# A constant mask written once a layer, and five pieces of work placed sooner at the seams of a three-stage kernel

## The reference

```
qkv = shift(x) @ wqkv;  q, k = l2norm, scale, rotate        # 8 heads of 64
sim[i, j] = q_i . k_j, and -max where i < j                 # causal mask
x = x + softmax(sim) @ v @ wo
h = layernorm(shift(x)) @ w1 + b1                           # 256 -> 2 * 682
x = x + (a * gelu(g)) @ w2 + b2                             # 682 -> 256
```

## Time and profile before

| what | value |
|---|---|
| time, median of 3 runs | 2665.61 us (2664.37 to 2666.09) |
| the profiled execution | 2666.19 us; its span 2664.4 us |
| mean granted TensorE clock | 0.992 |
| busy: PE, PEld, DVE, ACT, POOL | 97%, 84%, 72%, 64%, 54% |
| PE idle over the span | 73.7 us |

### The profile page before, as it was taken

The page is one execution under the profiler, slowest core; times in us unless marked ns, Lnnn a source line. Parts: engine busy times, 40 slices in busy tenths (PEclk is TensorE's granted clock), DMA queues, the critical chain, the costliest instruction groups (busy, mean ns, idle before and its releaser), DMA issues.

```text
span 2664.4 us, 71388 instructions
## 1 busy us (share of the span) xinstructions
PE 2590.7 (97%) x25088; PEld 2225.2 (84%) x25088; DVE 1919.9 (72%) x3779; ACT 1703.1 (64%) x4184; POOL 1426.1 (54%) x1512
## 2 busy tenths in 40 slices
PE   7999999979999999999999998999999999999998
PEld 5888888768888888887888887888888888888887
DVE  7777777668888778786555556887788887666664
ACT  4666666658778777774444445877777877444442
POOL 7888888567777776662000006777777665000000
PEclk9999999989999999999999999999999999999999
DMA  2111111111111111112111111111111111222221
GB/s 48 37 48 38 43 38 35 42 45 39 50 41 47 41 39 38 57 50 70 56 49 59 53 36 43 40 49 41 49 39 39 40 59 36 79 76 74 78 77 40
DMA packets 167250, 130.39 MB, mean 49 GB/s; under 512 B 24870, under 2 KB 165320, under 8 KB 167093
## 3 DMA queue, kind: packets, MB, share of 16 engines
q1 hardware_dynamic: 164789, 119.81, 14.7%
q0 software_dynamic: 2304, 8.47, 1.1%
HBM read 77.47 MB, written 50.33 MB: 48 GB/s over the span
## 4 chain that ended last, share of the span: by engine, by line
PE 70%; DVE 12%; ACT 11%; issue 5%; POOL 1%; DMA 1%; DVEq 0%; ACTq 0%; SPq 0%; POOLq 0%
ACT attn_E L1103 8%; PE const_banks L1393 6%; PE const_banks L1394 6%; PE const_banks L1395 6%; PE const_banks L1401 3%; PE const_banks L1403 3%; PE const_banks L1402 3%; DVE attn_neg_top L1305 3%; DVE attn_ss L1295 3%; DVE attn_rot_b L1276 3%; PE const_banks L1416 3%; PE const_banks L1415 3%; PE const_banks L1414 3%; PE const_banks L510 3%; PE const_banks L525 3%
## 5 line engine op out<-in xcount | busy, mean ns | idle before, releaser
L1103 ACT ACTIVATE attn_E<-const_banks,attn_nbias,attn_rn 128x128 f32<-128x128 f32 x1024 | 453.5, 462 | 135.7 <-DVE attn_nbias L1310 135.7
L1014 POOL TENSOR_TENSOR attn_qk<-attn_rot_a,attn_rot_b 128x1024 f32<-128x1024 f32 x128 | 303.6, 2372 | 348.9 <-issue 296.7
L1001 POOL TENSOR_TENSOR ffn_rstd<-ffn_var,const_neg_half 128x4 f32<-128x4 f32 x32 | 32.3, 1010 | 669.5 <-DVE ffn_var L1200 669.5
L1401 PE MATMUL const_banks<-weights_w_hi,attn_xT_hi 128*128 128x512 f32 x768 | 316.2, 412 | 4.9 <-ACT attn_sq L1138 4.6
L1403 PE MATMUL const_banks<-weights_w_hi,attn_xT_lo 128*128 128x512 f32 x768 | 304.9, 397 | 0.0
L1402 PE MATMUL const_banks<-weights_w_lo,attn_xT_hi 128*128 128x512 f32 x768 | 304.6, 397 | 0.0
L1221 DVE SCALAR_TENSOR_TENSOR ffn_gated<-const_banks,weights_b_col,ffn_gate 128x512 f32<-128x512 f32 (+1 forms) x192 | 143.7, 748 | 213.7 <-ACT ffn_gate L1081 206.9
L1393 PE MATMUL const_banks<-ffn_xT_hi,ffn_w_hi 128*128 128x512 f32 x704 | 282.2, 401 | 3.4 <-DVE ffn_gated L1221 3.4
L1394 PE MATMUL const_banks<-ffn_xT_lo,ffn_w_hi 128*128 128x512 f32 x704 | 278.7, 396 | 0.0
L1395 PE MATMUL const_banks<-ffn_xT_hi,ffn_w_lo 128*128 128x512 f32 x704 | 278.3, 395 | 0.0
L1081 ACT ACTIVATE ffn_gate<-const_banks,weights_b_col 128x512 f32<-128x512 f32 x160 | 110.3, 689 | 217.4 <-PE const_banks L1395 217.1
(11 more groups left out here) (179 smaller groups left out, 8001.9 us busy)
## 6 DMA issues: line engine op xcount, KB each, us to landing
attn_x_res<-xa SPq DMA_DIRECT2D x128, 128.0 KB, 4.8
xb<-attn_x_new SPq DMA_DIRECT2D x128, 128.0 KB, 1.7
ffn_x_<-xb SPq DMA_DIRECT2D x128, 128.0 KB
h<-ident_h SPq DMA_DIRECT2D x64, 128.0 KB, 1.7
xa<-ident_n SPq DMA_DIRECT2D x64, 128.0 KB, 1.7
attn_x_<-xa SPq DMA_DIRECT2D x128, 64.0 KB
xa<-ffn_x_new SPq DMA_DIRECT2D x16, 512.0 KB, 3.3
ffn_add<-h SPq DMA_DIRECT2D x16, 512.0 KB, 5.0
```

The lines of the kernel that those rows point to most:

```text
L1014: pool.tensor_tensor(qk[:, slot].rearrange("p a n -> p (a n)"), rot_a[:].rearrange("p a h d -> p (a h d)"), rot_b[:].rearrange("p a h d -> ...
L1103: last = act.activation(E[:, r, i], ps_s[:, r, i * P:(i + 1) * P], ACT.Exp, bias=nbias[:, r, i:i + 1], scale=rn[:, slot, h:h + 1], accum_o ...
L1401: pe.matmul(out_, xT_hi[:, slot, k], w.w_hi[:, k, cols], start=(k == 0), stop=False)
```

## The change

Six edits. (1) The mask for queries 0 to 63 is written in full (4 x 128 keys) only in step 2 of a layer; in all later steps only the first 64 keys of each head are written again. (2) On POOL in layer 0, `late(76)` moves from ahead of step 2 into step 1, between the products of the keys (L1025) and the power for the queries (L1027), so ahead of the load of w1. (3) Row 3 of layer 1 is loaded in the feed-forward step GROUPS + 1, with row 2. (4) The second group's statistics, its `group_rstd` and its normalisation are placed in attention steps 64, 65 and 66. (5) `row_out` goes through the blocks in `ORDER` and for its first row waits for four pieces at its head, and for the fifth and the sixth where they are used. (6) Its last matmul is now the `h_lo` product of block 4.

```diff
-                if on(0) and not (layer and step in (0, 1, 2)):
+                if on(0) and not (layer and step in (0, 1, 2, 3)):
                     load_row(sp, layer, t, i, u)
...
-                    for row in (first, first + 1) if step == GROUPS else (first + 2,):
+                    for row in (first, first + 1) if step == GROUPS else (first + 2, first + 3):
                         load_row(sp, layer + 1, row, row // 4, row % 4)
...
-        def attention_pool(pool, layer, before=None):
+        def attention_pool(pool, layer, before=None, within=None):
...
+                    if within and step == 1:
+                        within()
                     pool.tensor_tensor(rn[:, slot, 0:HEADS], ssm[:, 0:HEADS], c["neg_half"][:, 0:HEADS], ALU.pow
                                        ).then_inc(s["rn_done"], 1)
...
                 if step == ROWS - 2:
                     group_rstd(pool, layer * GROUPS)
+                if step == ROWS + 1:
+                    group_rstd(pool, layer * GROUPS + 1)
...
-                if on(0) and step != 0:
+                if on(0) and step not in (0, 1):
                     group_rstd(pool, t)
...
+                if step == ROWS:
+                    group_statistics(dve, layer * GROUPS + 1, layer * GROUPS // 4, 1)
+                if step == ROWS + 2:
+                    group_normalise(dve, layer * GROUPS + 1, 1)
...
-                        if p == 0:
+                        if p == 0 and step != 1:
                             group_statistics(dve, t, i, u)
-                        if p == 1:
+                        if p == 1 and step != 1:
                             group_normalise(dve, t, u)
...
-            if r == 0:
-                need(pe, f["h_lo"], KH * (t - 1))
             tok = slice(r * P, (r + 1) * P)
-            for k in range(FULL):
-                pe.matmul(dst, h_hi[:, slot, k, tok], w.w2_hi[:, k], start=(k == 0), stop=False)
+            for p, k in enumerate(ORDER):
+                if r == 0 and p >= KH - 2:
+                    need(pe, f["h_lo"], KH * (t - 2) + p + 1)
+                elif r == 0 and p == 0:
+                    need(pe, f["h_lo"], KH * (t - 1) - 2)
+                if k == FULL:
+                    pe.matmul(dst, h_tail[:, slot, tok], w.w2_hi[:, FULL], start=False, stop=False)
+                    pe.matmul(dst, h_tail[:, slot, tok], w.w2_lo[:, FULL], start=False, stop=False)
+                    continue
+                pe.matmul(dst, h_hi[:, slot, k, tok], w.w2_hi[:, k], start=(p == 0), stop=False)
...
+                        if step == 2:
+                            pe.matmul(ps_s[0:HD, r], eye, rule.rearrange("p i n -> p (i n)"),
+                                      start=True, stop=False, skip_group_check=True)
+                        else:
+                            pe.matmul(ps_s[0:HD, r].rearrange("p (i n) -> p i n", n=P)[:, :, 0:HD], eye,
+                                      rule[:, :, 0:HD], start=True, stop=False, skip_group_check=True)
...
-                attention_pool(pool, 0, between(late, STEPS, also))
+                attention_pool(pool, 0, between(late, {**STEPS, 2: ()}, also), lambda: late(ROWS + 12))
```

More of the change, by code:

```diff
@@ L1409, in row_out @@
             need(pe, f["sum_done"], j - 1)
-            if r == 0:
-                need(pe, f["h_lo"], KH * (t - 1))
             tok = slice(r * P, (r + 1) * P)
-            for k in range(FULL):
-                pe.matmul(dst, h_hi[:, slot, k, tok], w.w2_hi[:, k], start=(k == 0), stop=False)
+            for p, k in enumerate(ORDER):
[8 more added lines that the diff above has]
+                pe.matmul(dst, h_hi[:, slot, k, tok], w.w2_hi[:, k], start=(p == 0), stop=False)
                 pe.matmul(dst, h_hi[:, slot, k, tok], w.w2_lo[:, k], start=False, stop=False)
-                pe.matmul(dst, h_lo[:, slot, k, tok], w.w2_hi[:, k], start=False, stop=False)
-            pe.matmul(dst, h_tail[:, slot, tok], w.w2_hi[:, FULL], start=False, stop=False)
-            pe.matmul(dst, h_tail[:, slot, tok], w.w2_lo[:, FULL], start=False, stop=True).then_inc(f["out_ps"], 1)
+                last = pe.matmul(dst, h_lo[:, slot, k, tok], w.w2_hi[:, k], start=False, stop=(p == KH - 1))
+            last.then_inc(f["out_ps"], 1)
         def queries_keys(pe, b, slot):
@@ L1528, in body @@
                         eye, rule = c["ident_b"][own, own], c["causal"][own]
-                        pe.matmul(ps_s[0:HD, r], eye, rule.rearrange("p i n -> p (i n)"),
-                                  start=True, stop=False, skip_group_check=True)
+                        if step == 2:
[4 more added lines that the diff above has]
+                                      rule[:, :, 0:HD], start=True, stop=False, skip_group_check=True)
                         pe.matmul(ps_s[HD:P, r].rearrange("p (i n) -> p i n", n=P)[:, :, HD:P], eye, rule[:, :, 0:HD],
```

## The result

The kernel after takes 2650.9 us in the median (2646.3 to 2653.52, 5 runs), the kernel before on the same chip 2665.95 (2664.37 to 2666.89, 5 runs): ratio 0.9945 (0.9933 to 0.9956), 14.7 us faster, with 12 to 18 as the interval. The prediction was 2645, its range 2633 to 2656. The profiled execution took 2650.90 us with a span of 2649.1; PE is busy for 2582.9 us, so its idle time fell from 73.7 to 66.2 us. That is about half of the gain; most of the rest is clock: the mean granted clock rose from 0.992 to 0.994, and 0.002 of the span is some 5 us.

What follows compares the result with a forecast made beforehand. PE was taken to bound the kernel, busy 97% of the span, with waits and low-clock stretches at the seams. Terms 0 + 5.0 + 4.0 + 6.5 + 1.7 + 3.1 = 20.3 us off 2666.2 gave 2645 after median adjustment, range 2633 to 2656.

Steps and rivals of the forecast that it cites:

- Edit 1: Attention rows' mask of queries 0 to 63: shortening it priced at 0 us, at most 13.
- The long mask lies beside that chain: Attention rows: the mask of queries 0 to 63 is hidden by the longer-running products of queries 64 to 127; 0 us.
- Edit 2: Start of layer 0's attention: POOL reaches the last row's work 4.4 us sooner; gain 5.0 us, bounds 1.2 and 6.0.
- Edit 3: Start of layer 1's attention: PE's 3.67 us wait for row 3's load goes; gain 4.0 us, bounds 2.0 and 5.3.
- Edit 4: Attention to feed-forward: PE's waits for the second group's statistics and normalisation go; 6.5 us in layer 0, 1.7 in layer 1.
- Edits 5 and 6: Kernel's end: most of PE's 3.04 us wait before the last `row_out` is filled; gain 3.1 us, bounds 1.5 and 3.4.
- M: Rival, attention rows: the mask is on PE's path and pays 13 us as well, 2632 us; chance 0.12.
- rival A: At the seams: half the gain is taken back by the next limit, 9.6 us won, 2656 us; chance 0.17.
- a seam's wait comes back under another name: At the seams: a sign that the forecast is wrong, a removed wait reappearing with another cause; no size given.
- the likeliest case: Whole kernel: the summed gain of 20.3 us holds, 2645 us, own range 2640 to 2651; chance 0.62.
- S: Rival, hardware loop: overhead of the looped rows grows; if doubled it costs 28 us, 2673 us; chance 0.03.
- N: Rival, whole kernel: an unseen wait takes up the gains wholly, 2663 us; chance 0.06.

Runs made afterwards that it cites:

- mask_only: The halved mask of queries 0 to 63 (edit 1) alone on the kernel before: 2662.79 us against 2664.33, ratio 0.9992.
- the long mask twice: Kernel before with the mask matmul of queries 0 to 63 (512 columns) issued twice in every row: 2671.34 us, ratio 1.0021.
- the short mask twice: Kernel before with the mask matmul of queries 64 to 127 (256 columns) issued twice in every row: 2665.7 us, ratio 1.0004.
- edit 4 alone: Only the second group's statistics and normalisation moved into attention's last steps, on the kernel before: 2658.1 us, ratio 0.9978.
- the load behind: Kernel after with layer 0's first load of w1 one step later on POOL, behind step 2's powers: 2646.99 us, ratio 0.9934.

## Why the prediction was right, and where it was off

The time is in the range and 5.9 us above the number. By parts:

- **Edit 1, 0.** Right in value, by a reason that is only half right: mask_only's row is 10.04 against 10.05, which by 126 rows is 1 to 2 us, and the interval of its 2.1 us includes zero. "The long mask lies beside that chain" is where it was weak: the tiles are coupled, as the long mask twice shows, but only after one product (two records), and the single long mask was short enough. And a longer chain did not cost what the prediction's account of it implies: 13.7 us were expected of the short mask twice and 1.1 (-1.3 to 3.7) measured. What hides an op of 0.1 us here is not the neighbouring tile alone, but also the slack of the row behind it.
- **Edit 2, 5.0; measured about 1** (0.6 to 1.1 in the trace once the late trace before is allowed for, 1.6 (-1.1 to 4.0) alone). This term failed: even its lower bound, 1.2, is hardly reached. The queue was followed rightly: L293 at 554.34, L1409 at 559.58, L1014 at 561.51 (forecast 554.7, 560, near 562). The failing step is "following each engine's queue by its present durations": L1301's present duration is 0.17 and it took 3.24, since in its new place it runs beside L1014. The Trainium skill (SBUF — State Buffer, Who interferes with whom) says that a DVE instruction with two SBUF inputs contends with a GpSimd instruction that reads SBUF; the ends at 563.96 and 563.92 agree with it, and so do 560.52 and 560.49. The clock adds to it: from 566 to 576 it was 0.66 in the kernel after, behind the 2.9 us wait.
- **Edit 3, 4.0; 4.2 in the trace, 6.1 (3.7 to 8.5) alone.** The wait went, and one of the two low stretches behind it; 1600 to 1650 has 0.97 of the clock in place of 0.93.
- **Edit 4, 6.5 in layer 0; 1.7 in the trace, 3.5 in that of edit 4 alone.** This and edit 2 are the terms that made the difference. The seam itself won 6.9 us, as forecast, but the step didn't ask what is late next: the sum was made up to 1227 and the next group, 14 us on, not looked at. Before, the third group's statistics started at 1236.36 with no wait for a load and PE had work; with the work before them some 8 us sooner, the loads and the slow normalisation became the path, and 5.2 us went back: PE's wait of 2.92 us and, from 1240.6, a stretch at the low clock (0.79 from 1238 to 1246). A small part too: of the 1.71 us wait for `ffn_gated`, 0.69 is left, because the split, now sooner, holds L1343 for 2.78 us ahead of it on DVE; the prediction saw the hold and looked only at who uses the low part, not at what is queued behind it. In layer 1, with nothing to split, edit 4 alone gives 1.9 against the forecast 1.7; the 2.9 in the kernel after has another 0.9 from a low stretch at 2248 that is in the trace before and not in this one.
- **Edits 5 and 6, 3.1; 3.1 in both traces, and 3.5 (1.1 to 5.9) alone.** The waits forecast as about 1.0 and 0.4 are 0.87 and 0.18, with no low stretch after them.

So rival A holds in its mechanism, a seam won and given back at the next limit, for two of the six terms: the sign "a seam's wait comes back under another name" was seen twice. The total, 14.7 us, lies midway between the likeliest case (20.3) and A (9.6). Some of it is luck. Edit 2 and edit 4 in layer 0 are short by some 9 us in the trace; what makes up for part of it is not in the sum: steady rows (1.4 us, in part edit 1's), the late trace before (1.3 to 1.8), and a low stretch less in layer 1 (0.9). S and N fell: the rows of the loop did not get longer, and the time did change. M fell with mask_only.

The kernel after spreads over 7.2 us (2646.3 to 2653.52) and before over 2.5. The granted clock of its five runs goes with the time: 0.996 at 2646.3, 0.994 at 2650.75 and 2650.9, 0.992 and 0.993 at 2651.92 and 2653.52; 0.001 of the span is 2.6 us. That the runs differ by a low stretch more or less is argued from the clock alone, and not tested.

## What to carry to other kernels

When a seam gets sooner by several us, go on past it to the next work that has not moved with it, here loads that are issued only after the previous stage; the gain is worth what that work allows. A duration read from a trace is good only for its neighbours: an operation of DVE moved beside one of POOL has to be costed anew, and so does one left in place when POOL's work is moved next to it. Before a saving in a busy engine's steady state is priced in full, double the operation and see what the loop takes.

## What the runs showed of the hardware

- Tiles of the array run ahead of the program's order, but not far: with a tile held by a second mask, the other stopped after two records (one float32 product) until 0.46 us after the masks began, when the held tile started its first product.
- A DVE addition of 128x16, 0.17 us otherwise, took 3.24 us beside POOL and ended 0.04 us after POOL's L1014. It had started 0.8 us before L1014, while POOL issued the last of the four transfers; whether those hold it too is open. With the load behind, another DVE operation with two inputs in SBUF (L1261, 128x512, at 565.76) ran beside such issues of POOL and took its usual 0.69 us, which speaks against it.
- Four DVE normalisations take 1.4 us alone and 5.7 us beside POOL's split of 128x1536; whichever of the two is off the path should wait.
- A loop in which PE is busy for 99.7% of the time took in 0.11 us more of PE's work in each row and grew by 0.02.
